# A last group written out: scores ahead of outputs, three outputs in other banks, a last norm on VectorE

## The reference

```python
xn = layernorm(x, g_in)
q = (xn @ Wq).reshape(b, n, H, DH).transpose(0, 2, 1, 3) * scale
k, v = split(xn @ Wkv)            # and the null key, null value in front
sim = where(causal & mask, einsum('bhid,bjd->bhij', q, k) + bias, -max)
out = einsum('bhij,bjd->bhid', softmax(sim), v)
out = out.transpose(0, 2, 1, 3).reshape(b, n, INNER) @ Wo
return x + layernorm(out, g_out)
```

## Time and profile before

| | us |
|---|---|
| median of 3 runs | 1084.39 (1083.17 to 1084.90) |
| span of the profiled execution | 1081.3 |
| PE busy in the span | 1028.3 (95%) |
| POOL busy | 831.5 (77%) |
| DVE busy | 766.1 (71%) |
| ACT busy | 660.8 (61%) |
| last output of PE ends (batch 63) | 1072.8 |

### The profile page before, as it was taken

How to read it: one execution, slowest core, us unless ns; L and a number is a source line. 1 busy time by engine, 2 the same in 40 slices (tenths; PEclk the granted TensorE clock), 3 DMA queues, 4 the chain that set the end, 5 groups by cost and what they waited for, 6 DMA issues and landing times.

```text
span 1081.3 us, 42925 instructions
## 1 busy us (share of the span) xinstructions
PE 1028.3 (95%) x14224; PEld 902.0 (83%) x14224; DVE 766.1 (71%) x3517; ACT 660.8 (61%) x2617; POOL 831.5 (77%) x1488
## 2 busy tenths in 40 slices
PE   4769999999999999999999999999999999999974
PEld 3668888888888888888888888888888888888853
DVE  4667777777777777777777777777777867776551
ACT  4546756656675665667566566656656765665551
POOL 1758787887888788788878878877788887877773
PEclk9889999999999999999999999999999999999987
DMA  7312222232222222222222222222322222221101
GB/s 216 103 45 70 83 82 85 72 92 64 73 84 84 79 76 89 63 76 83 83 73 85 71 71 84 84 83 68 91 72 68 82 86 82 70 70 51 46 26 39
DMA packets 90013, 84.01 MB, mean 78 GB/s; under 512 B 21568, under 2 KB 64064, under 8 KB 89792
## 3 DMA queue, kind: packets, MB, share of 16 engines
q1 hardware_dynamic: 87680, 78.97, 24.1%
q10 hardware_dynamic: 2112, 2.10, 0.6%
HBM read 40.11 MB, written 16.78 MB: 53 GB/s over the span
## 4 chain that ended last, share of the span: by engine, by line
PE 92%; POOL 1%; DVE 1%; SPq 1%; issue 1%; ACT 1%; DMA 0%; POOLq 0%; DVEq 0%; ACTq 0%
PE ps_proj L482 39%; PE ps_pv L476 35%; PE ps_s L439 10%; PE ps_pv L463 9%; SPq L331 1%; DVE wq_lo L649 0%; POOL bias_b L884 0%; POOL w_nrm L893 0%; DVE o_lo L567 0%; ACT xn L780 0%; POOL wo_lo L962 0%; DVE y_stats L575 0%; ACT o_hi L761 0%; DMA x_split<-xn 0%; POOL small L917 0%
## 5 line engine op out<-in xcount | busy, mean ns | idle before, releaser
L753 ACT ACTIVATE exp_bot<-logit_bot,neg_max 128x129 f32<-128x129 f32 x512 | 201.6, 398 | 256.7 <-DVE neg_max L546 233.7
L884 POOL TENSOR_TENSOR bias_b<-bias_c,mask_add 128x256 f32<-128x256 f32 (+1 forms) x512 | 293.6, 603 | 41.9 <-DVE neg_max L546 41.4
L482 PE MATMUL ps_proj<-xt_hi,wq_hi 128*128 128x256 f32 x1024 | 302.5, 295 | 4.1 <-DVE q_sb L627 2.7
L482 PE MATMUL ps_proj<-xt_hi,wq_lo 128*128 128x256 f32 x1024 | 289.0, 282 | 0.0
L482 PE MATMUL ps_proj<-xt_lo,wq_hi 128*128 128x256 f32 x1024 | 288.7, 282 | 0.0
L546 DVE CUSTOM_DVE_ANT_0 logit_bot<-ps_s,bias_b 128x128 f32<-128x128 f32 x512 | 128.4, 289 | 187.8 <-PE ps_s L439 162.6
L476 PE MATMUL ps_pv<-wo_hi,o_hi 128*128 128x512 f32 x512 | 212.2, 414 | 12.7 <-DVE o_lo L567 12.7
L893 POOL TENSOR_TENSOR w_nrm<-exp_bot,w_inv 128x256 f32<-128x256 f32 x256 | 156.7, 612 | 72.7 <-DVE w_inv L555 71.7
L482 PEld LDWEIGHTS ps_proj<-xt_hi,wq_hi 128*128 128x128 f32 x1024 | 193.6, 189 | 19.2 <-issue 10.3
L476 PE MATMUL ps_pv<-wo_lo,o_hi 128*128 128x512 f32 x512 | 205.2, 401 | 0.0
L476 PE MATMUL ps_pv<-wo_hi,o_lo 128*128 128x512 f32 x512 | 204.9, 400 | 0.0
(11 more groups left out here) (64 smaller groups left out, 1747.4 us busy)
## 6 DMA issues: line engine op xcount, KB each, us to landing
x_in<-in_x_dram SPq DMA_DIRECT2D x32, 512.0 KB, 4.2
x_res<-in_x_dram SPq DMA_DIRECT2D x64, 256.0 KB, 3.4
out_dram<-y_out SPq DMA_DIRECT2D x64, 256.0 KB, 2.1
x_split<-xn SPq DMA_DIRECT2D x480, 32.0 KB, 1.9
v_rep<-v_raw SPq DMA_DIRECT2D x256, 32.0 KB, 1.9
w_raw<-in_L_cond_Wq_dram ACTq DMA_DIRECT2D x4, 512.0 KB, 7.9
w_raw<-in_L_cond_Wo_dram SPq DMA_DIRECT2D x4, 512.0 KB, 4.9
mask_u<-in_mask_BxS_bk_dram SPq DMA_DIRECT2D x32, 32.0 KB, 3.9
```

Of the source, the lines that this page charges most:

```text
L482: mm = pe.matmul(ps[:, 0:TOK], w[:, k, cols], xt[:, slot, k], start=(j == 0), stop=(j == len(todo) - 1))
L753: ins = nc.scalar.activation(out_[:, s, j], in_[:, s, j], ACT.Exp, bias=neg_max[:, s, k:k + 1], scale=-1.0, accum_out=w_sum[:, s, k:k + 1])
L884: ins = nc.gpsimd.tensor_tensor(out_, bias, key_mask, ALU.add)
```

## The change

The last eight steps of the last pair and the five after them are taken out of the step loop. Every engine has a function `last_group` with its order written out. In it:

- PE makes `scores(12)` ahead of output 61, and `scores(14)` between its two halves; `values(63)` stands between the halves of output 62. `project_out` is cut into `project_out_half`.
- The outputs go to other banks: 61 to `ps_proj[0]`, 62 to `ps_proj[1]`, 63 to `ps_s[0]`, in place of `ps_pv[0]`. From batch 62 on, `values` does not wait for the norm of the batch before, but `pow` on POOL does.
- Batch 62's heads are written to slot 0 of `xt_hi` and `xt_lo`, free by then, so that heads 63 need not wait for output 62.
- The norm of batch 63 is two passes on DVE: (output - mean) x `g_out`, then x 1/std + `x_res`. POOL makes only 1/std.
- On POOL, `masked_bias` and `normalize` are grouped anew and `residual(60)` stands behind the last `normalize`. On ACT, the exponentials of head 10 stand ahead of the heads of 61, and the norms of 61 and 62 around the heads of 63. On DVE, `logits(11)` stands ahead of the heads of 61, and the statistics of 61 behind all softmax work and ahead of the heads of 62.

```diff
-PLAN_63 = PLAN | {"add": 8}
-TAIL = 5
+        o_of, ps_o_of = {}, {B - 3: ps_proj[0], B - 2: ps_proj[1], B - 1: ps_s[0]}
...
         def steps(last):
-            return range(CP + (TAIL if last else 0))
+            return range(CG if last else CP)
...
+        def outs_before_heads(batch):
+            return batch - 1 if isinstance(batch, int) and batch >= B_LAST else batch
...
+        o_of[B - 2] = as_heads(xt_hi), as_heads(xt_lo)
...
 # PE
-                wait(pe, y_nrm_made, batch)
+                if not (isinstance(batch, int) and batch >= B_LAST):
+                    wait(pe, y_nrm_made, batch)
...
+            def last_group(p):
+                scores(p, CG)
+                front(F_LAST, 1, "q", 6)
+                front(F_LAST, 1, "q", 7)
+                scores(p, CG + 2)
+                values(p, B_LAST - 1, 1)
+                scores(p, CG + 4)
+                pe.wait_ge(q_made, QT * GROUPS)
+                project_out_half(B_LAST - 1, 0)
+                scores(p, CG + 6)
+                project_out_half(B_LAST - 1, 1)
+                values(p, B_LAST, 2)
+                project_out_half(B_LAST, 0)
+                values(p, B_LAST + 1, 3)
+                project_out_half(B_LAST, 1)
+                pe.wait_ge(s_read, 2 * CP * PAIRS)
+                project_out(B_LAST + 1)
...
 # DVE, after the statistics of 60, q6 and q7 (turn(t): transposed of heads t and t + 1)
+                turn(-2)
+                inverse(N_LAST, CG)
+                logits(N_LAST + 2, CG + 2)
+                inverse(N_LAST + 1, CG + 1)
+                logits(N_LAST + 3, CG + 3)
+                heads(B_LAST - 1)
+                turn(0)
+                inverse(N_LAST + 2, CG + 2)
+                spread_v_of(F_LAST, 1)
+                logits(N_LAST + 4, CG + 4)
+                inverse(N_LAST + 3, CG + 3)
+                logits(N_LAST + 5, CG + 5)
+                turn(2)
+                inverse(N_LAST + 4, CG + 4)
+                logits(N_LAST + 6, CG + 6)
+                inverse(N_LAST + 5, CG + 5)
+                logits(N_LAST + 7, CG + 7)
+                turn(4)
+                inverse(N_LAST + 6, CG + 6)
+                inverse(N_LAST + 7, CG + 7)
+                out_stats(B_LAST - 1, 1)
+                out_mean_var(B_LAST - 1, 1)
+                heads(B_LAST)
+                turn(6)
+                heads(B_LAST + 1)
+                out_stats(B_LAST, 2)
+                out_mean_var(B_LAST, 2)
+                dve.wait_ge(y_shift_made, B_LAST)
+                out_stats(B_LAST + 1, 3)
+                out_mean_var(B_LAST + 1, 3)
+                last_out()
+
+            def last_out():
+                b = (B - 1) % GB
+                dve.wait_ge(y_mv_made, B)
+                dve.wait_ge(y_out_made, B_LAST)
+                nc.vector.scalar_tensor_tensor(out=y_nrm[:, b], in0=out_bank(B - 1)[:], scalar=y_mv[:, b, 0:1],
+                                               in1=gout_row[:], op0=ALU.subtract, op1=ALU.mult).then_inc(last_g_made, 1)
...
+                nc.vector.scalar_tensor_tensor(out=y_out[:, b], in0=y_nrm[:, b], scalar=y_rstd[:, b:b + 1],
+                                               in1=x_res[:, b], op0=ALU.mult, op1=ALU.add).then_inc(last_out_made, 1)
...
 # ACT
+                soft(0)
+                out_norm(B_LAST - 2, 0)
+                soft(1)
+                soft(2)
+                heads(B_LAST - 1)
+                for t in range(3, CG):
+                    soft(t)
+                heads(B_LAST)
+                out_norm(B_LAST - 1, 1)
+                heads(B_LAST + 1)
+                out_norm(B_LAST, 2)
...
 # POOL (bias(t), normal(t): masked_bias and normalize of head 8 + t)
+                bias(2)
+                y_scale(B_LAST - 2, 0)
+                bias(3)
+                normal(0)
+                normal(1)
+                bias(4)
+                bias(5)
+                normal(2)
+                normal(3)
+                bias(6)
+                bias(7)
+                for t in range(4, CG):
+                    normal(t)
+                residual(B_LAST - 2, 0)
+                y_scale(B_LAST - 1, 1)
+                residual(B_LAST - 1, 1)
+                y_scale(B_LAST, 2)
+                residual(B_LAST, 2)
+                y_rstd_of(B - 1, 3)
```

More of the change, by code:

```diff
@@ L264, in due @@
             for back in range(-3, 4):
-                plan = PLAN_63 if last and back == 3 else PLAN
-                if 4 * back + plan[what] == t and not (first and back < 0):
+                if 4 * back + PLAN[what] == t and not (first and back < 0):
                     yield 2 * GB * p + back, back
@@ L766, in out_norm @@
                 wait(act, y_shift_made, batch + 1)
-                nc.scalar.activation(y_nrm[:, b], ps_o[:], ACT.Identity, bias=y_shift[:, b:b + 1],
+                nc.scalar.activation(y_nrm[:, b], out_bank(batch)[:], ACT.Identity, bias=y_shift[:, b:b + 1],
                                      scale=y_rstd[:, b:b + 1]).then_inc(y_nrm_made, 1)
@@ L870, in body, with last_group, soft, heads @@
                             x_norm(f, k)
+                if last:
+                    last_group()
+            def last_group():
+                def soft(t):
+                    exponentials(N_LAST + t, CG + t, 1)
+                    exponentials(N_LAST + t, CG + t, 0)
+                def heads(batch):
+                    for g in range(4):
+                        heads_hi(batch, g)
+                soft(0)
[9 more added lines that the diff above has]
+                out_norm(B_LAST, 2)
             run_pairs_ahead(act, body)
@@ L909, in x_rstd_of, with y_rstd_of @@
                 nc.gpsimd.tensor_tensor(x_shift[:], x_mr[:], minus_one[:], ALU.mult).then_inc(x_shift_made, 1)
[L911 removed]
+            def y_rstd_of(batch, back):
                 b = back % GB
@@ L916, in y_scale @@
                 wait(pool, y_var_made, batch + 1)
+                if isinstance(batch, int) and batch >= B_LAST:
+                    wait(pool, y_nrm_made, batch - 1)
                 nc.gpsimd.tensor_tensor(y_rstd[:, c], y_var[:, c], pow_col[:, 0:1], ALU.pow).then_inc(y_rstd_made, 1)
+            def y_scale(batch, back):
+                b = back % GB
+                c = slice(b, b + 1)
+                y_rstd_of(batch, back)
                 wait(pool, y_rstd_made, batch + 1)
@@ L989, in body, with last_group, bias, normal @@
                         first_extras[t]()
+                if last:
+                    last_group()
+            def last_group():
+                def bias(t):
+                    masked_bias(N_LAST + t, F_LAST, CG + t)
+                def normal(t):
+                    normalize(N_LAST + t, CG + t)
+                bias(2)
[17 more added lines that the diff above has]
+                y_rstd_of(B - 1, 3)
             run_pairs_ahead(pool, body)
```

67 lines of the change are left out of this document (53 added, 14 removed).

## The result

The changed kernel took 1068.87 us (median of 4 runs, 1066.18 to 1070.32) beside 1083.78 us for the kernel before, timed with it: a ratio of 0.9859, with a 95% interval from 0.9843 to 0.9875. That is 14.9 us less. The forecast was 1071.2.

The account below looks back on a forecast made before the run. PE's work bounds the kernel up to about 1030 us, with waits and clock falls after. Span 1081.3 less 15.6 (3.5, 8.5, 0.5, 3.1) gives 1065.7; plus 2.5 clock and 3.1 span-to-time, 1071.2 us; range 1067 to 1076.

Parts of the forecast that it names:

- The bound and the timetable: From about 1030 us: softmax chain sets the pace, then PE from output 62 on; dated steps, 15.6 us saved before clock loss.
- The early scores: scores(12) and scores(14) on PE moved ahead, so values(62) ends 3.5 us earlier.
- The banks: Other output banks remove PE's waits around values(63): 8.5 us less from the end of values(62) to that of values(63).
- The late residuals: POOL's residuals moved later, residual(60) after all normalize; residual(62) done 0.9 us before POOL is wanted for batch 63.
- The last norm: Batch 63's norm on DVE: 1.75 us from aggregate to y_out instead of 4.87, 3.1 us less.
- The clock: PE's clock falls to half after the 3.0 us hole ahead of output 62, costing 2.5 us.
- Case A: The timetable as worked out, with a clock fall at the hole ahead of output 62: 1071.2 us, chance 49%.
- B: The hole ahead of output 62 leaves PE's clock full: 1068.8 us, chance 25%.
- D: PE's clock is down from the first half of output 61 to the end: 1081 us, chance 3%.
- C: Softmax chain slower through handoffs, or clock falls before scores(14): 3 to 4 us more, 1074.5 us, chance 17%.
- E: Slower: x_res loads, issued only after the late residuals, decide the end: 1085 us or more, chance 3%.
- F: No effect: something ahead of the last group, not PE's order, sets the end: 1084.4 us, chance 3%.

Follow-up runs that it names:

- e4: Changed kernel with batch 62's heads back in the shared o_hi and o_lo instead of the free slot of x; 1072.53 us, ratio 0.9891.
- e5: Changed kernel with scores 12 and scores 14 back behind output 61 on PE; 1077.30 us, ratio 0.9929.
- e3: Changed kernel with batch 62's output bank, its heads' place and values(63) behind both halves of output 62 put back; 1077.69 us, ratio 0.9933.
- e1: Changed kernel with only the last norm put back to ACT and POOL; 1071.89 us, ratio 0.9888.
- e2: Kernel before with only the last norm moved to two DVE passes; 1081.21 us, ratio 0.9973.
- e6: Changed kernel with 11 matmuls of unread result added on PE in the hole ahead of output 62; 1069.08 us, ratio 0.9851.
- e7: Changed kernel with DVE's statistics of batch 61 moved behind the heads of 62; 1068.47 us, ratio 0.9854.
- e11: As e8, with the heads of batch 61 ahead of head 10's exponentials on ACT; 1068.10 us, ratio 0.9836.
- e8: Changed kernel with heads 62 ahead of head 15's exponentials, statistics of 61 behind heads 62, residual(60) ahead of the last normalize; 1068.50 us, ratio 0.9847.
- e10: Repeat of e8, timed beside the changed kernel on one chip; 1068.67 us, ratio 0.9844.
- e12: As e11, with 4 unread matmuls ahead of scores 14 and 6 ahead of output 62 on PE; 1066.96 us, ratio 0.9844.

## Why the prediction was right

| step | forecast | measured (less 0.46) |
|---|---|---|
| `scores(12)` starts | 1032.85 | 1033.07 |
| output 61 starts | 1034.6 | 1034.67 |
| `scores(14)` starts | 1038.9 | 1038.52 |
| `values(62)` ends | 1044.3 | 1044.0 |
| hole ahead of output 62 | 3.0 | 2.90 |
| lost to the clock | 2.5 | 1.5 |
| aggregate to `y_out` | 1.75 | 1.74 |
| span | 1068.2 | 1067.0 |

**The bound and the timetable** held: the softmax chain sets the pace until output 62, PE from there on, and the dates of the table came within 0.4 us. Within the chain the forecast dated the heads of 62 by POOL's queue, and rightly: `normalize(13)` was to end at 1043.05 and ended at 1042.8 (less 0.46). The link is one head earlier than written, as head 14's exponentials waited 1.5 us for POOL and head 15's followed with no wait. `scores(14)`, among its own signs, does not stand on that path: in e4 it came 0.65 us late with no effect on output 62. The recorded text also reads the clock row too kindly: it has 8 in its second and third slice too, and the page has PE less busy there. Both kernels share that part, so nothing of the sum hangs on it. **The early scores** do feed the chain (e5), though their price is not parted from the clock's. **The banks** held, as e3 shows for bank, place and order of output 62 together, and so did **the place of heads 62** (e4), once the clock is taken out. **The late residuals** cost nothing: `residual(62)` ended at 1062.45, 0.84 us before POOL was wanted, forecast as 0.9. **The last norm** held (e1, e2), and the price of a 128x512 pass, for which the trace had no row, was 0.75 us.

**Where the sizes were off.** The clock: the loss of 2.5 us was 1.45 (e6). The clock fell only 1.1 us after output 62 had begun and was back 3.4 us later; the forecast took 1.7 to 2.9 us from the 3.4 and 5.7 us of slow work of before, and the measured loss lies just under that. Why it came back sooner than after the first fall of before is not shown. Case A, a fall here, is the one that occurred. But the length of the hole alone does not decide it. Four profiles with the hole of 2.9 us ahead of output 62 have the fall, and so has e5 at one of 2.4 us ahead of output 61; two with 2.2 us (e4, e7) have not, and of three with 1.5 us one has. The step from span to time: 3.1 us were added, from the median of the timed runs and one profile's span. In every run here in which both are known, of one execution, the time is 1.8 to 2.2 us above the span. Together these are 2.1 of the 2.3 us by which 1071.2 was too high. That the rest is only 0.2 us is luck: the starts of single executions differ by more than 3 us.

**The rivals.** B, the clock at full throughout, gave 1068.8, nearer to the measured 1068.87 than A. That is chance: the clock did fall, in both profiles of the changed kernel, and B's number also has the 3.1 us in it. With the clock kept up (e6) the tail is 1.45 us shorter still. D, the clock down from output 61 on, did not occur: the waits of 0.8, 0.7 and 0.8 us left it at 1.00 in the changed kernel. The Trainium skill ("TensorE: Matmul & The Clock Gate", section "HAM oscillation — how this bites in real kernels") says that after a long enough idle stretch the next burst starts at the lower rate. The traces agree only in part: behind the long holes the clock did fall, but 1.1 us into output 62 in the changed kernel (0.2 when it was run again), and before the change 1.3 us after `scores(14)` and 0.6 us after `values(63)` had begun. The fall in e4, behind waits of 0.8 and 0.7 us, is not what that section describes. C, a slower chain, is refuted by the table; its other form, a fall of the clock ahead of `scores(14)`, came in e4 and cost nothing at output 62, not 3 to 4 us. E did not occur. F falls with e1 to e5.

What stays open: what makes the clock fall at a hole of 1.5 us in e11 and not in e8 and e10, and in e4's output 61 but in none of the eight other profiles with the same work and waits there. The starts of e8, e10 and e11 differed by up to 1.3 us at `scores(10)`, but no run here varied that alone. Open too is what the regrouping on POOL, ACT and DVE gives by itself.

## What to carry to other kernels

A kernel whose steady state is bound by PE can still lose some 15 us where the pipeline runs dry. There the order on each queue decides, and here a timetable with the durations of the trace foretold it within half a microsecond. Start what feeds the longest chain before the work that fills PE, and give the last outputs banks and buffers that are idle by then. Look for the queue that really holds the path: a date that looks decisive, as `scores(14)` here, can have time to spare. A hole on PE can cost twice, by its length and by the clock behind it; in e6, matmuls whose result is overwritten won back the second part.

## What the runs showed that was not expected

- The start is less steady than the rest: the same instructions reached the kernel's fourth `scores` between 54.4 and 58.5 us, more than what any of the new orders of e6 to e12 gained. Compared from a common event on, in the profile, the tails of the two orders that were profiled twice agreed within 0.1 us, where times of one kernel differ by 2 to 5.
- A fall of the clock need not cost anything: in e4, 3.4 us at 0.50 in output 61 made `scores(14)` 0.65 us late but not output 62, since `logits(14)` would have waited for POOL anyway.
- With ten useless matmuls added the kernel's tail was 1.0 us shorter (e12 beside e11, one profile each, with a fall of the clock in e11 and none in e12).
